# Compressed branch of the first attention: block masks on TensorE, copies out of PSUM on ScalarE, VectorE begins with the maxima

## The reference, cut to what matters

```python
csim = jnp.einsum('bhgnd,bhjd->bhgnj', q, ck) * SCALE
ck_last = jnp.concatenate([jnp.array([-1]), (jnp.arange(nc) + 1) * CBLK - 1])
cmask = ck_last[None, :] < jnp.arange(n)[:, None]
csim = jnp.where(cmask, csim, NEG)
c_out = jnp.einsum('bhgnj,bhjd->bhgnd', jax.nn.softmax(csim, -1), cv)
imp = csim[..., 1:].mean(axis=2)
imp = jnp.concatenate([jnp.full(imp.shape[:-1] + (1,), -1000.0, imp.dtype), imp], axis=-1)
imp = jax.nn.softmax(imp, -1)[..., 1:]
sel_vals, sel_idx = jax.lax.top_k(imp, NSEL)
```

## Time and profile before

| | |
|---|---|
| median of 3 runs | 4815.79 us |
| the profiled execution, its own time | 4769.71 us |
| span of the profiled execution | 4767.9 us |
| TensorE matmul (PE) busy | 4140.7 us, 87% |
| VectorE (DVE) busy | 3325.1 us, 70% |
| ScalarE (ACT) busy | 2001.1 us, 42% |
| GpSimd (POOL) busy | 1443.2 us, 30% |
| mean granted TensorE clock | 0.936 of full |

### The profile page before, as it was taken

One profiled execution on the slowest core, in us unless ns is written; L12 is line 12 of the kernel. 1 busy time (PEld: TensorE's weight loads), 2 busy tenths in 40 slices (PEclk: granted clock), 3 DMA queues, 4 the chain that ended last, 5 costly groups with the idle time before them and its releaser, 6 DMA issues.

```text
span 4767.9 us, 72906 instructions
## 1 busy us (share of the span) xinstructions
PE 4140.7 (87%) x23550; PEld 2508.8 (53%) x23551; DVE 3325.1 (70%) x9356; ACT 2001.1 (42%) x4593; POOL 1443.2 (30%) x1227
## 2 busy tenths in 40 slices
PE   6788888888888897898878899899999999978996
PEld 3444444444444453785544455454545445548995
DVE  7877877878787884457746576867676776764555
ACT  1243434343434344222224455555554555443442
POOL 0000000000000001324005455656454655544553
PEclk7899998999999998999989999999999999989998
DMA  4121121212221113872126611112111211135666
GB/s 117 19 33 40 26 43 24 41 27 38 34 39 23 32 19 102 267 237 79 35 82 104 74 55 43 54 45 62 32 58 37 59 46 46 50 139 104 111 106 163
DMA packets 320320, 327.12 MB, mean 69 GB/s; under 512 B 160934, under 2 KB 253630, under 8 KB 318814
## 3 DMA queue, kind: packets, MB, share of 16 engines
q1 hardware_dynamic: 275898, 250.27, 20.7%
q0 software_dynamic: 39936, 70.87, 8.8%
q10 hardware_dynamic: 4112, 1.32, 0.2%
HBM read 182.60 MB, written 92.94 MB: 58 GB/s over the span
## 4 chain that ended last, share of the span: by engine, by line
PE 63%; DVE 25%; ACT 3%; issue 3%; DMA 3%; SPq 2%; POOL 2%; DVEq 0%; ACTq 0%; POOLq 0%
DVE a_mm L1239 7%; PE PS L2256 6%; PE PS L2271 6%; PE PS L2284 6%; PE PS L2769 5%; PE PS L2301 5%; PE PS L2314 4%; PE PS L833 3%; PE PS L2780 3%; PE PS L773 2%; PE PS L1724 2%; PE PS L800 2%; PE PS L636 2%; DVE PS L2581 1%; PE PS L811 1%
## 5 line engine op out<-in xcount | busy, mean ns | idle before, releaser
L1239 DVE TENSOR_REDUCE a_mm<-PS 128x2 f32<-128x384 f32 (+4 forms) x1152 | 673.7, 610 | 234.3 <-PE PS L777 232.8
L970 ACT ACTIVATE a_PT<-PS 128x512 f32<-128x512 f32 x896 | 514.2, 602 | 631.5 <-PE PS L811 412.8
L2654 POOL TENSOR_TENSOR d_ef<-d_ef,d_soft 128x768 f32<-128x768 f32 (+3 forms) x512 | 641.1, 1261 | 399.4 <-DVE d_soft L2590 397.2
L2362 ACT ACTIVATE d_ef<-PS,d_soft 128x128 f32<-128x128 f32 (+3 forms) x1024 | 530.5, 525 | 405.5 <-DVE d_soft L2590 347.2
L2581 DVE CUSTOM_DVE_ANT_0 PS<-PS,d_cmask 128x128 f32<-128x128 f32 (+3 forms) x1024 | 482.2, 512 | 277.9 <-PE PS L2271 276.1
L1425 POOL DMA_INDIRECT list<-a_tok,slots x64 | 62.8, 981 | 1621.5 <-ACT a_PT L970 1382.8
L2271 PE MATMUL PS<-W 64*128 64x128 f32 (+3 forms) x2048 | 421.5, 489 | 81.1 <-ACT d_ef L2362 63.9
L773 PE MATMUL PS<-a_K,a_Q 96*128 96x192 bf16 (+4 forms) x2048 | 424.7, 286 | 66.7 <-DVE a_mm L1239 33.0
L2284 PE MATMUL PS<-ident,d_ef 128*128 128x128 f32 x2560 | 391.7, 290 | 32.5 <-POOL d_ef L2654 31.2
L2284 PEld LDWEIGHTS PS<-ident,d_ef 128*128 128x128 f32 x2560 | 283.5, 145 | 235.1 <-issue 100.3
L773 PEld LDWEIGHTS PS<-a_K,a_Q 80*128 80x128 bf16 (+1 forms) x2048 | 181.6, 103 | 379.3 <-DVE a_mm L1239 104.4
(11 more groups left out here) (381 smaller groups left out, 7761.1 us busy)
## 6 DMA issues: line engine op xcount, KB each, us to landing
W<-W SPq DMA_DIRECT2D x768, 64.0 KB, 2.0
W<-in_exp SPq DMA_DIRECT2D x96, 384.0 KB, 4.5
e_xg<-xrow SPq DMA_DIRECT2D x144, 132.5 KB, 2.1
a_Q<-scr SPq DMA_DIRECT2D x384, 32.0 KB
yrow<-bc_ob SPq DMA_DIRECT2D x48, 256.0 KB, 5.5
W<-in_exp SPq DMA_DIRECT2D x16, 768.0 KB, 10.1
scr<-a_qsp SPq DMA_DIRECT2D x24, 384.0 KB, 3.0
acc<-in_zero POOLq DMA_DIRECT2D x34, 256.0 KB, 12.1
```

Of the source, the lines that this page charges most:

```text
L970: e.activation(PT[:, 4 * (n % 2) + q4, :], RS.of(("exp", n, q4))[:, :], ACT.Exp, scale=S0).then_inc(act.sem, act.mark(("exp", n, q4)))
L1239: e.tensor_reduce(mm[:, i % 2, kind, c:c + len(gs)], RP.of(("top", b, u, kind, gs[0]))[:, 0:len(gs) * n].rearrange("p (g k) -> p g k", g=l ...
L2362: e.activation(ef[:, n % 7, r, 0:nk], S.of(("exp", n))[:, r, 0:nk], ACT.Exp, scale=-1.0, bias=nm[:, n % 7, r:r + 1], accum_out=zz[:, n % 7 ...
L2654: e.tensor_tensor(ef[:, n % 7, :, 0:nk], ef[:, n % 7, :, 0:nk], zr[:, n % 7, :].unsqueeze(2).to_broadcast([128, 2, nk]), ALU.mult).then_in ...
```

## The change

The mask tile `maskc` becomes bf16. On TensorE each of the four `cs` matmuls leaves its group open, and a second matmul (identity times the mask, broadcast to 8 heads, 264 columns, bf16) adds the mask in the bank. The two `im` matmuls are followed by one such matmul of 256 columns. The banks are released by ScalarE. ScalarE gets the copies: in its first piece parts 0 and 1, in the second 2 and 3, in the third `im`; it still has four pieces before the wait for `im2`. VectorE does nothing in its first two pieces; its third begins with a wait for the fourth copy and the maximum L1165; the `yield 1` that stood between the `im` addition and this maximum is gone. The wait for the copy of `im` stands before L1171.

```diff
-    c["maskc"] = mc
+    c["maskc"] = mc.astype(bf)
-            maskc = sb("maskc", [128, 4, 33])
+            maskc = sb("maskc", [128, 4, 33], BF16)
@@ tensor: compressed
-                        p, old = RM.take(dve, ("cs", b, i, q4))
+                        p, old = RM.take(act, ("cs", b, i, q4))
                         vacate(e, old)
                         e.matmul(p[:, 0:264], qraw[:, x, qc], ckb[:, x, c:c + 8, :].rearrange("p a b -> p (a b)"),
-                                 start=True, stop=True).then_inc(pe.sem, pe.mark(("cs", b, i, q4)))
+                                 start=True, stop=False)
+                        e.matmul(p[:, 0:264].rearrange("p (u j) -> p u j", u=8), identb[:],
+                                 maskc[:, i, :].unsqueeze(1).to_broadcast([128, 8, 33]), start=False, stop=True
+                                 ).then_inc(pe.sem, pe.mark(("cs", b, i, q4)))
                         if q4 % 2:
                             yield
-                    p, old = RM.take(dve, ("im", b, i))
+                    p, old = RM.take(act, ("im", b, i))
                     vacate(e, old)
                     for x in range(2):
                         e.matmul(p[:, 128 * x:128 * x + 128], qraw[:, x, qc],
-                                 ckim[:, x, :, :].rearrange("p a b -> p (a b)"), start=True, stop=True
-                                 ).then_inc(pe.sem, pe.mark(("im", b, i)))
+                                 ckim[:, x, :, :].rearrange("p a b -> p (a b)"), start=(x == 0), stop=False)
+                    e.matmul(flat8(p[:, 0:256]), identb[:], maskc[:, i, 1:33].unsqueeze(1).to_broadcast([128, 8, 32]),
+                             start=False, stop=True).then_inc(pe.sem, pe.mark(("im", b, i)))
@@ scalar: compressed
-                    for _ in range(4):
-                        yield
+                    if b == 0 and i == 0:
+                        e.wait_ge(dve.sem, dve.at("im"))
+                    for q4 in range(4):
+                        e.wait_ge(pe.sem, pe.at(("cs", b, i, q4)))
+                        e.activation(cs[:, 8 * q4:8 * q4 + 8, :].rearrange("p u j -> p (u j)"),
+                                     RM.of(("cs", b, i, q4))[:, 0:264], ACT.Copy
+                                     ).then_inc(act.sem, act.mark(("cs", b, i, q4)))
+                        if q4 % 2:
+                            yield
+                    e.wait_ge(pe.sem, pe.at(("im", b, i)))
+                    e.activation(im[:, :, 1:33], flat8(RM.of(("im", b, i))[:, 0:256]), ACT.Copy
+                                 ).then_inc(act.sem, act.mark(("im", b, i)))
+                    yield
+                    yield
@@ vector: compressed
-                    if n:
-                        e.wait_ge(act.sem, act.at(("eC", (n - 1) // 4, (n - 1) % 4)))
-                    for q4 in range(4):
-                        if q4 % 2:
-                            yield 1
-                        e.wait_ge(pe.sem, pe.at(("cs", b, i, q4)))
-                        if q4 == 0:
-                            chain(e, dve)
-                        e.tensor_tensor(cs[:, 8 * q4:8 * q4 + 8, :],
-                                        RM.of(("cs", b, i, q4))[:, 0:264].rearrange("p (u j) -> p u j", u=8),
-                                        maskc[:, i, :].unsqueeze(1).to_broadcast([128, 8, 33]), ALU.add
-                                        ).then_inc(dve.sem, dve.mark(("cs", b, i, q4)))
-                        if q4 % 2:
-                            yield
-                    e.wait_ge(pe.sem, pe.at(("im", b, i)))
-                    e.tensor_tensor(im[:, :, 1:33], flat8(RM.of(("im", b, i))[:, 0:256]),
-                                    maskc[:, i, 1:33].unsqueeze(1).to_broadcast([128, 8, 32]), ALU.add
-                                    ).then_inc(dve.sem, dve.mark(("im", b, i)))
-                    yield 1
+                    yield
+                    yield
+                    e.wait_ge(act.sem, act.at(("cs", b, i, 3)))
                     chain(e, dve)
                     e.tensor_reduce(z4[:, 0, :], cs[:], AX, ALU.max).then_inc(dve.sem, dve.tick())
...
+                    e.wait_ge(act.sem, act.at(("im", b, i)))
                     e.tensor_reduce(z4[:, 1, 0:8], im[:], AX, ALU.max).then_inc(dve.sem, dve.tick())
...
-                e.memset(im[:], -4000.0).then_inc(dve.sem, dve.tick())
+                e.memset(im[:], -4000.0).then_inc(dve.sem, dve.mark("im"))
```

## The result

| | kernel before | changed kernel |
|---|---|---|
| median, same comparison | 4813.74 us (4803.59 to 4815.94) | 4747.6 us (4744.34 to 4750.11) |
| ratio | 1 | 0.9866 [0.9849, 0.9883] |
| profiled execution, span | 4769.71, 4767.9 us | 4747.82, 4746.1 us |
| stretch from 90 us to the last exponential of `im2` | 1635 us | 1575 us |

The change makes the kernel 66 us faster. The forecast was 25 us (4791), its lower bound 4755: right in sign, with less than half of the size.

What follows compares the result with a forecast made beforehand. The prediction took TensorE's waits around each tile, not any engine's busy time, as the bound: -44 us of waits plus 19 us of masks gave -25 us, from 4815.8 to 4791 us, range 4755 to 4825.

Steps and rivals of the forecast that it cites:

- TensorE's idle time in phase a: TensorE's waits around tiles of `compressed`: 6.3 us less a row, times 7 rows, 44 us gained.
- masks: 160 bf16 mask matmuls added to TensorE, 0.12 us each, all on the path: 19 us more.
- the bank waits: Tile i = 1: TensorE's 1.45 and 0.23 us waits for VectorE to empty a `cs` bank (1.68) would go.
- the fold's: Tile i = 1: TensorE's 1.02 us wait for a fold queued on VectorE behind maximum L1165 would go.
- the late exponential in tile i = 1: TensorE's 1.26 us wait for a score exponential after ScalarE's `im2` wait; about half would remain.
- The rival of dear masks: Between fp32 matmuls on TensorE, bf16 masks don't stream: 0.51 us each, +37 us, 4853 us; chance 0.12.
- neither busy time is the bound: From 90 to 1745 us, TensorE (85% busy) and VectorE (80%) take turns; TensorE's waits count, 66.8 us in seven rows.
- the clock gives more: Shorter TensorE waits avoid 44 us of low clock, 22 us more gain: 4769 us; chance 0.22, shared with whole pool going.
- some 1.1 us earlier: Maximum L1165 ahead of the probe on VectorE brings the `im2` mark 1.1 us earlier, shortening ScalarE's wait by as much.
- This is no gain by itself: The 66.1 us of additions taken off VectorE, 2.1 us a tile, give nothing alone, since VectorE waits longer for TensorE.
- Taken back: TensorE meets the next place where VectorE is late; half of the 44 us idles again: 4813 us; chance 0.16.
- ScalarE late: In every second place a ScalarE copy delays an exponential by its length: 31 us back, 4822 us; chance 0.08.

Runs made afterwards that it cites:

- experiment 3: The changed kernel with the 160 added mask matmuls left out: 4672.14 us, 28 us under the changed kernel on the same chip.
- the twelfth kernel: The changed kernel with scratch additions of the old sizes on VectorE and maximum L1165 back behind the probe: 4801.65 us, 0.9976 of the kernel before.
- experiments 8 and 11: The changed kernel plus VectorE scratch additions of the old sizes in the old places, run twice: 4788.08 and 4788.79 us, 0.9957 and 0.9956 of the kernel before.

## Why the prediction was too small

| term | forecast | measured |
|---|---|---|
| TensorE's idle time in phase a | -44 | -50 |
| masks | +19 | +26 to +28 |
| TensorE's busy time otherwise | 0 | -36 |
| sum | -25 | -60 in the stretch, -58 at phase a's end, -55 to -66 timed |

**The idle time: right.** -44 was forecast from four tiles, and 247.8 - 198.0 = 50 us went, 5 of them in the first row (42.6 to 37.7 us). The distribution was less right: the bank waits and the fold's are gone as written, but the late exponential in tile i = 1 stayed (1.26, now 1.22 us), and the first row, for which I counted nothing, ran 3 to 9 us faster from its first to its fifth `im2` exponential (180.8 and 182.4 us in the two profiles of before, 177.5, 173.3 and 176.3 in the three of after).

**The masks: mis-sized in effect.** 0.12 us each were forecast from a stream of bf16 matmuls, 0.16 to 0.18 is what leaving them out gave back; the trace of the changed kernel shows that the step alone is not the whole. From the mask to the next scores the step is 746.77 - 746.65 = 0.12 us in the timeline above, just as forecast, at full clock. The 17 us of experiment 3 are about that price; the other 9 are busy time that the low clock made longer, as far as one pair of profiles shows it. The rival of dear masks (0.51 us each, decisive from 0.275) fell.

**The step that failed: "neither busy time is the bound. What counts is each wait of TensorE around a tile".** The sum holds TensorE's busy time fixed but for the masks. It fell by 36 us beside them: the busy time shown fell by 10 from before to after, and 26 of new work lie in it. Two things are hidden in that figure.

- *Clock.* By the records of the granted clock, 276 and 281 us of the stretch lie at the low level in the two profiles of the kernel before, 248, 250 and 254 in the three of the changed one, 28 less. TensorE was busy for 240 and 244 of these us before and for 212, 214 and 219 after, some 28 less: at half speed that is 14 us. This was my rival "the clock gives more", at 44 us of such time and 22 us of gain. It came, at two thirds of that size, and together with the forecast, not in its place. The rule of the Trainium skill (page "TensorE: Matmul & The Clock Gate", section "A second HAM failure mode: psum-queue depth-cycling"), that pauses for PSUM banks make the clock swing and cost throughput, has the direction right for this pair: fewer pauses, 28 us less at the low level. It tells the size of neither, and it does not order all runs: the twelfth kernel waits less than the kernel before (226.1 us against 247.8) and has 300 us at the low level.
- *What a wait costs beyond its bracket.* The rows of matmuls overlap (the mask's is 0.28 us long, and the next begins after 0.12), but at a wait a row stands in its full length. In the earlier trace rows the two records of L718 stand as 0.71 us: from 766.09 to the wait of 0.23 us that ends at 767.03. In the changed kernel the same two records take 0.44 us, from 746.21 to the mask at 746.65 (the timeline above), at the same full clock. So this wait cost 0.27 us more than its 0.23, and that stands as busy time. L718 waited for the additions of L1153 in 31 places of the stretch, 16.2 us in all, and for their successors in none. The row of the kernel before is below. Over all rows, TensorE was idle before 340 matmul records before and 275 after. At full clock the mean step from a record of L718 to the next matmul, idle time taken off, is 268 ns before, 238 without masks and 228 in the changed kernel, some 250 records.

```profile
PE PS L718 <- DVE a_cs L1153: 16.2, 31, 1.5
```

Together (an estimate, with the busy time at the low level counted at half, which fits L718's 228 and 458 ns a record at the two levels): TensorE's work at full clock was 1267 us in both profiles of the kernel before, 1271 to 1272 in the three of the changed one and 1255 without masks. So of the 10 us by which busy time fell, 14 are the clock, 17 were added by the masks, and 13 fell away beside. About half of the 13 stands behind L718 and L725, where the bank waits were; that the rest went with waits too is likely, as 65 of them are gone, but not shown. The 36 us are these 14 and 13, and the 9 us of clock in the masks' 26.

The waits of weight loads are no measure of this. Their total for VectorE fell from 426.7 to 366.1 us, 61 less, where the matmul rows show 196.5 and 163.9, 33 less; but a weight load also waits while TensorE works, as at 755.26 above.

**The order was undercounted.** I gave the moved maximum "some 1.1 us earlier", acting through ScalarE's wait. The run with the order alone shows ScalarE's wait down only from 136.0 to 111.2 us and yet 31 us of phase a gained; TensorE's idle time fell by 24 of them (247.8 to 223.5) and its busy time by 7. In the changed kernel without the order it is at 95.4 us and 21 us are gained. So the wait for `im2` does not measure the gain. The order took 25 us off it and gave 31 of phase a, the rest of the change took 41 off and gave 21. What is likely, by the place of the idle time, though no run times it by itself: in the old place the 1.25 us maximum stood behind a probe's maximum and ahead of all that VectorE does next; in the new one it fills the time in which VectorE waited for that probe. 31 us / 32 tiles is 1 us a tile, nearly the 1.12 us of idle time of the earlier trace rows, and not only where I saw an exponential come late. Per row (rows 1 to 7) the step from tile 0's `im2` exponential to tile 1's shrinks by 1.1 us with the order alone, 1 to 2 by 1.2, 2 to 3 by 0.5, 3 to the next row's 0 by 1.6 (48.9, 27.9, 34.5, 111.4 to 47.8, 26.7, 34.0, 109.8).

**"This is no gain by itself": wrong.** Of the 66 us taken off VectorE I counted only what a visible wait would return. The load is worth 18 to 36 us with the order (experiments 8 and 11) and 15 to 21 without it. VectorE waits for TensorE for 225 us in sum, but at many places it is the late one, and 2 us less a tile makes it less late there.

**The base.** The sum was right to go by the profiled execution, and carrying the 46 us over to the median was right too: 4815.8 - 58 would have been 4758, and 4747.6 came, the rest being the spread between comparisons (55 to 66).

**The other rivals.** *Taken back* fell: TensorE's idle time fell in full, and row by row (from row 1 on, the mean time from a tile's `im2` exponential to that of the same tile a row later is 223.5 us before, 215.1 after). *ScalarE late* fell: the 160 copies take 62.4 us (391 ns and 384 ns each, forecast 390), and the waits of matmul rows for ScalarE fell from 43.5 to 28.7 us.

**The signs that I named.** L718's waits gone: yes. L1165 within 0.5 us of the fourth copy: 0.43 and yes, though in 17 tiles it waits for the copy. ScalarE's wait down by 30 or more: by 72. Masks stepping by 0.11 to 0.15: 0.12 in the row above. ScalarE +62, VectorE -66: +57 and -60. The rest as long as before: no, its second phase was not, for a reason of its own. Phase a 25 us earlier: 58.

## What to carry to other kernels

- When two engines take turns, don't sum only the idle time in front of matmul rows. Compare the length of the row at a wait with that of the same row in a stream (0.71 against 0.44 us here), and read the time at the low clock: here 36 of 60 us lay in "busy" time of TensorE.
- Ask of each long instruction on the helper engine whether a short one, for which TensorE waits, is queued behind it. Moving one maximum a piece ahead, a deleted line, gave 35 us; the whole offload with its masks gave 28 us. Don't carry such a figure over to another state of the kernel: with the masks added and VectorE as busy as before, the same move gave 10 to 13.
- The price of added work depends on who is late: 160 mask matmuls cost nothing measurable in the timing while VectorE was late, 28 us once it was relieved. After an offload such work is worth trimming: 39% fewer mask columns gave 18 us more.

## What the runs showed of the hardware

**A second phase of two lengths.** In the profiled executions the second phase (its gathers by GpSimd, its matmuls; no line of it differs) takes 592 to 595 us in the first profile of before and on one chip (four runs), and 642 to 648 us in the first profile of after and on two other chips (eight runs). The medians of the kernel before follow: 4755 us on the first chip, 4812 and 4809 on the other two. The profile on which the prediction rested is of the short kind, and the runs beside it (4803.59 to 4815.94) are as slow as those of the long kind. That would account for the 46 us between profile and median; the second phase of the executions without a profile is not on record. It does explain why the first pair of profiles differs by 22 us where the timings differ by 66. Waits of the changed kernel in its second phase (1809 to 2454 us), and the same 100 us around the burst of gathers, kernel before and after:

```profile
ACT W L1783 <- remote: 41.3, 4, 21.3
```

```profile
2164.00:2264.00 100.00, 81.08 (x292) 51.89 (x291) 72.58 (x149) 23.25 (x49) 43.80 (x45) 0.93 0.26 76
```

```profile
2105.00:2205.00 100.00, 56.82 (x191) 36.31 (x192) 48.39 (x99) 15.68 (x30) 36.03 (x37) 0.78 0.22 62
```

In the long profile shown ScalarE waits up to 21.3 us for something that the profile can't name, while GpSimd issues its gathers back to back, as it does in the short kind too, TensorE is busy 57 instead of 81 us of 100, and the clock drops to 0.78. None of the short profiles has such a wait. What holds the update up, and why on some chips alone, stays open.

**The third phase varies by 20 us.** Phase d, from its first instruction to its last, took 1807 to 1828 us over the fourteen profiles, with no line of it changed: 1807, 1811 and 1812 in those of the changed kernel, 1815 and 1828 in those of the kernel before. Whether a few us of the gain lie there is not shown. Differences of 10 us between two profiled executions say nothing here, and in phase a the same kernel differs by up to 9 us from chip to chip.
